# Two P V products of one head group joined into one block on TensorE, and two tile moves exchanged between ScalarE and VectorE

## The reference

```python
q = _layer_norm(query, ln1_g, ln1_b)
qh = (q @ wq + bq); kh = (context @ wk + bk); vh = (context @ wv + bv)
scores = jnp.einsum('bqhd,bkhd->bhqk', qh, kh) * scale
scores = jnp.where(allowed, scores, NEG_INF)        # causal
probs = jax.nn.softmax(scores, axis=-1)
o = jnp.einsum('bhqk,bkhd->bqhd', probs, vh)
x = query + o @ wo + bo
ff = jax.nn.gelu(_layer_norm(x) @ w1 + b1, approximate=False) @ w2 + b2
return x + ff
```

## Time and profile before

| what | value |
|---|---|
| median of 3 runs | 2777.89 us (2776.44 to 2778.57) |
| the profiled execution's own time | 2778.07 us |
| its span | 2776.2 us |
| PE, PEld (its weight loads), DVE, ACT, POOL busy | 98%, 90%, 74%, 60%, 32% |
| granted clock of PE over the span | 0.995 of full speed |

### The profile page before, as it was taken

The page is one execution under the profiler, slowest core; times in us unless marked ns, Lnnn a source line. Parts: engine busy times, 40 slices in busy tenths (PEclk is TensorE's granted clock), DMA queues, the critical chain, the costliest instruction groups (busy, mean ns, idle before and its releaser), DMA issues.

```text
span 2776.2 us, 67352 instructions
## 1 busy us (share of the span) xinstructions
PE 2730.1 (98%) x21928; PEld 2489.3 (90%) x21928; DVE 2041.0 (74%) x5205; ACT 1654.4 (60%) x4017; POOL 893.4 (32%) x842
## 2 busy tenths in 40 slices
PE   7999999999999999999979999999998999999999
PEld 6888888888888888888869999999998999999999
DVE  6777777777777777777698787787788566566556
ACT  5766667666676666766665656656556445444444
POOL 6657566575765656656510000000000000000000
PEclk9999999999999999999999999999999999999999
DMA  5233333333333323333243533534435433343342
GB/s 186 104 126 132 118 118 118 129 131 111 121 117 129 133 106 125 121 130 124 100 163 130 196 146 148 196 135 160 191 126 197 160 145 141 129 166 136 122 157 99
DMA packets 153084, 383.58 MB, mean 138 GB/s; under 512 B 13440, under 2 KB 17536, under 8 KB 144768
## 3 DMA queue, kind: packets, MB, share of 16 engines
q1 hardware_dynamic: 152960, 382.28, 37.1%
HBM read 172.51 MB, written 109.05 MB: 101 GB/s over the span
## 4 chain that ended last, share of the span: by engine, by line
PE 94%; DVE 2%; issue 2%; POOL 1%; ACT 1%; DMA 0%; SPq 0%; DVEq 0%; POOLq 0%; ACTq 0%
PE bank_d L495 19%; PE bank_t L525 11%; PE bank_s L1299 7%; PE bank_d L490 7%; PE bank_s L1300 6%; PE bank_s L1301 6%; PE bank_s L510 6%; PE bank_v L548 5%; PE bank_d L1299 5%; PE bank_d L1301 5%; PE bank_d L1300 5%; PE bank_v L1299 2%; PE bank_v L1300 2%; PE bank_v L1301 2%; PE bank_t L1299 1%
## 5 line engine op out<-in xcount | busy, mean ns | idle before, releaser
L862 ACT ACTIVATE sm<-sm,mins 128x128 f32<-128x128 f32 (+3 forms) x1024 | 572.0, 559 | 439.2 <-DVE mins L670 434.6
L989 POOL TENSOR_SCALAR sm<-sm,recips 128x128 f32<-128x128 f32 (+3 forms) x512 | 549.8, 1084 | 235.9 <-DVE recips L682 234.1
L670 DVE CUSTOM_DVE_ANT_0 sm<-bank_s,mask 128x128 f32<-128x128 f32 (+3 forms) x1024 | 474.3, 484 | 66.8 <-PE bank_s L510 64.0
L615 DVE COPY pT<-bank_t 128x384 f32<-128x384 f32 (+1 forms) x544 | 306.8, 564 | 210.6 <-PE bank_t L525 208.5
L1299 PE MATMUL bank_s<-w_hi,a_hi 128*128 128x256 f32 x1536 | 435.6, 284 | 2.1 <-DVE a_lo L1425 2.1
L1300 PE MATMUL bank_s<-w_lo,a_hi 128*128 128x256 f32 x1536 | 435.0, 283 | 0.0
L1301 PE MATMUL bank_s<-w_hi,a_lo 128*128 128x256 f32 x1536 | 434.9, 283 | 0.0
L525 PE MATMUL bank_t<-ident,sm 128*128 128x128 f32 x2560 | 412.8, 275 | 10.5 <-POOL sm L989 3.4
L525 PEld LDWEIGHTS bank_t<-ident,sm 128*128 128x128 f32 x2560 | 306.6, 140 | 92.3 <-issue 32.7
L1299 PE MATMUL bank_d<-b_hi,w_hi 128*128 128x256 f32 x1280 | 369.8, 289 | 14.0 <-ACT g L1726 7.7
L1301 PE MATMUL bank_d<-b_hi,w_lo 128*128 128x256 f32 x1280 | 364.3, 285 | 0.0
(11 more groups left out here) (161 smaller groups left out, 6550.2 us busy)
## 6 DMA issues: line engine op xcount, KB each, us to landing
stack<-st_hi SPq DMA_DIRECT2D x256, 256.0 KB, 2.4
stack<-st_lo SPq DMA_DIRECT2D x128, 256.0 KB, 2.4
xr<-x_scratch SPq DMA_DIRECT2D x64, 512.0 KB, 4.2
b_scratch<-b_hi SPq DMA_DIRECT2D x16, 1792.0 KB, 9.1
b_scratch<-b_lo SPq DMA_DIRECT2D x16, 1792.0 KB, 12.8
b_hi<-b_scratch SPq DMA_DIRECT2D x16, 1792.0 KB, 7.3
b_lo<-b_scratch SPq DMA_DIRECT2D x16, 1792.0 KB, 11.2
xt<-in_x SPq DMA_DIRECT2D x64, 256.0 KB, 2.7
```

The source lines that it names most:

```text
L615: copy(out, src).then_inc(moved[n % 2], 1)
L670: op = V.tensor_tensor_reduce(sm[:, n % SLOTS_S, off:off + w], bank_s[n % BANKS_S][:, off:off + w], mask[:, 512 - w:512], 1.0, 0.0, ALU.ad ...
L862: op = A.activation(row, row, ACT.Exp, bias=mins[:, g % 2, c:c + 1], scale=-1.0, accum_out=sums[:, g % 2, c:c + 1])
L989: op = G_.tensor_scalar(out=row, in0=row, scalar1=recips[:, g % 2, c:c + 1], scalar2=None, op0=ALU.mult)
```

## The change

P V of the second group leaves its two places. Both pairs are now done one after the other in step 3 of the third group (n = 27), after K3 and ahead of the transposes of tile 24. Steps 21 and 29 have no P V any more. The last tile of that group, tile 11 (n = 23, 512 columns), is moved in step 27 by DVE and no more by ACT; its tile 3 (n = 15, 384 columns) is moved in step 19 by ACT and no more by DVE. All other groups stay as they are.

```diff
-ACT_MOVES = [(5, 9, 11), (5, 9, 11), (3, 5, 7, 9, 11), (5, 9, 11)]
+ACT_MOVES = [(5, 9, 11), (3, 5, 9), (3, 5, 7, 9, 11), (5, 9, 11)]
...
-    R_AT, PV1_AT, PV0_AT, O_PROD_AT, O_HIGH_AT, O_HIGH_LATE = 4, 5, 9, 6, 7, 11
+    R_AT, PV1_AT, PV0_AT, PV_AT, O_PROD_AT, O_HIGH_AT, O_HIGH_LATE = 4, 5, 9, 3, 6, 7, 11
...
-                    if k == PV1_AT and not (it.first and g == 0):
+
+                    if k == PV_AT and g == 2:
+                        pv(it, g - 1, 0)
                         pv(it, g - 1, 1)
-                    if k == PV0_AT and not it.tail:
+                    if k == PV1_AT and g != 2 and not (it.first and g == 0):
+                        pv(it, g - 1, 1)
+                    if k == PV0_AT and g != 1 and not it.tail:
                         pv(it, g, 0)
                     if n >= LAG and not it.tail or n < LAG and not it.first:
                         p_transpose(it, n - LAG)
```

## The result

The changed kernel takes 2785.85 us (median of 8 runs, 2785.22 to 2790.05), the kernel before, run beside it, 2777.0 (8 runs, 2774.25 to 2778.57). The ratio is 1.0038, with a 95% interval of 1.003 to 1.0047: slower, by 8.9 us in the medians, where 9.4 had been forecast. The profiled executions lie 10.0 apart (2788.08 and 2778.07, spans 2786.2 and 2776.2).

A forecast was written before the change was run, and what follows sets the result against it. PE sets the pace (86.26 of 86.35 us a batch busy). 8.1 for batches 1 to 14, 1.5 for batch 0 and -0.2 for batch 15 give 9.4 on 2778.07, about 2787.3 us, 0.34% slower; range 2774.5 to 2792.

The forecast's parts named there:

- PE's own work: P V of both pairs: one joined block costs 2.445 us in place of 2.73, so PE alone gains 0.285 a batch.
- The moves exchanged at no cost: Steps 19 and 27: ACT's extra move (about 0.5) and DVE's (0.69) both fall into idle time and add nothing.
- Tile 24 late: Behind the joined block in step 27: the transposes of tile 24 come at 427.165 in place of 425.70.
- DVE's queue: From step 28: everything behind tile 24's move shifts by 1.465; the moves from tile 26 to tile 32's mask are 1.08 late.
- ACT's exponential of tile 32: It waits for DVE's mask of tile 32 and starts at 437.34 in place of 436.70, 0.64 late.
- DVE's `x_low` of X2: It waits for ACT's `x_high` of X2, so what follows it in DVE's queue is 0.64 late.
- the moves of tile 30 and 34: DVE's move of tile 30 and mask of tile 34, each 0.64 late, hold PE's transposes of tile 32 and scores of step 36.
- 0.58 a batch: Scores of step 36 start 0.52 to 0.64 later, taken as 0.58; over batches 1 to 14 it makes 8.1.
- Batch 0: 1.5 forecast: POOL's scalings hold PE in group 1, so emptying step 21 frees nothing: 0.58 + 0.93 = 1.5 lost.
- Batch 15: -0.2 forecast: No X blocks or statistics there, so at most 0.28 is gained, partly lost in PE's waits in its last group: -0.2.
- waits of 0.6 in L525 and 0.2 in L510: New PE waits for DVE in steps 35 and 36, on the move of `pT` and the mask, some 14 of each.
- The rival of the kept gain: The joined block's gain stays and DVE and ACT catch up unseen: -3.5 in all, 2774.4 us, chance 0.18.

The follow-up runs named there:

- join_stats3: The changed kernel with the next batch's fourth layer-norm statistics (about 1.15 us of DVE) in step 27 in place of step 28: 2773.43 us, 0.9987 of the kernel before.
- join_stats3_split: The changed kernel with the fourth statistics in step 27 and tile 24's transposes between P V of pair 0 and pair 1: 2776.63 us, 1.0006 of the kernel before.
- moves_only: The kernel before with only the two exchanged tile moves of the changed kernel, P V in its old places: 2774.8 us, 0.9996 of the kernel before.
- join_act26: The changed kernel with tile 26 of the third group moved by ACT in step 30 in place of DVE: 2782.68 us, 1.002 of the kernel before.
- stats3_only: The kernel before with only the fourth statistics in step 27 in place of step 28: 2776.03 us, 0.9999 of the kernel before.
- join_oldmoves: The changed kernel with the moves of tiles 3 and 11 given back to their former engines: 2789.24 us, 1.0042 of the kernel before.
- join_stats3_b0: The changed kernel with the fourth statistics in step 27 and batch 0's P V of pair 0 back in step 21: 2773.11 us, 0.9987 of the kernel before.

## Why the prediction was right, point by point

- **PE's own work: right.** Joined block 2.30, edges 0.33 and 0.30, step 21 shorter by 0.95. The mean period of join_stats3 over batches 1 to 14, where nothing stalls, is 86.07 against 86.37: the gain of 0.28 to 0.30 a batch is real, and join_stats3_split, which has the two switches back, loses it again.
- **The moves exchanged at no cost: right** for the time (moves_only).
- **Tile 24 late, DVE's queue, ACT's exponential of tile 32, DVE's `x_low` of X2, the moves of tile 30 and 34: right in each link.** 3.11 of idle time were expected as "nearly 3". The steps of the chain stand in the trace in the order and with the distances that were summed. Counted from the last product of step 21, the mask of tile 32 is 1.11 late (summed: 1.08), the exponential of tile 32 0.67, `x_low` of X2 and the move of tile 30 0.66 (0.64 each), the scores of tile 36 0.60 (0.58). Taking work off that chain (1.15 in join_stats3, 0.46 in join_act26) takes the loss away wholly and in part, though tile 24 is transposed as late as in the changed kernel. A rival in which PE would suffer from tile 24's lateness directly is excluded by this.
- **0.58 a batch: right in this place, short in the sum.** In batch 4 it is 0.60, and from the scores of step 21 to those of step 36 it is 0.61 in the mean of batches 1 to 14, 8.5 in all. The whole loss of these batches is 9.33 (from the joined block of batch 1, 166.59, to that of batch 15, 1385.10, against 154.78 to 1363.96 for P V in step 21 before), where 8.1 was forecast. Of the rest, 0.3 comes between step 36 and the end of the batch, 0.02 a batch; the kernels with the stall have it, join_stats3 doesn't, and what makes it is open. The other 0.5 lies in steps 0 to 2 and can't be told from scatter. There, PE's scores in step 2 wait up to 0.2 for DVE's mask, in different batches of each trace. From the list of waits, first the changed kernel and then the kernel before:

```profile
PEld bank_s L510 <- DVE mins L674: 0.4, 2, 0.2
```

```profile
PEld bank_s L510 <- DVE mins L670: 0.4, 2, 0.2
```

  These are batches 9 and 12 of the changed kernel, 2 and 14 of the kernel before. From the first scores of a batch to those of step 3, the 14 batches take 85.6 in all before and 86.1 in the changed kernel, but also 85.5 in moves_only and 86.2 in stats3_only, which lose nothing.
- **A reading of the kernel before was too smooth.** The periods of its batches 1 to 14 lie between 86.31 and 86.55, not within 0.1 of each other, and its weight loads do wait for DVE in the two places just shown. The sum by one batch held all the same, as batch 4 (86.33) has none of these waits.
- **Batch 0: 1.5 forecast, 1.4 measured.** From its first P V to the block of batch 1 it is 116.74 (49.85 to 166.59), before 104.50 to P V in step 21 and 10.81 from there to where the block would start. POOL's scaling held PE as said: PE's waits for it took over the place of the product that had left: from the scores of step 21 to those of step 22 it is 0.38 shorter, from there to those of step 27 0.33 longer.
- **Batch 15: -0.2 forecast, -0.27 measured** (34.18 from the block to the last P V of the stage, against 34.45).
- **Together:** 1.43 + 9.33 - 0.27 = 10.5 by the trace, against 9.4, of which an earlier start of this execution (49.85 against 50.28) takes 0.4, so that the two profiled executions differ by 10.0. The term that was too small is that of batches 1 to 14, by 1.2: 0.4 in the stall itself, 0.3 behind step 36, 0.5 in waits that scatter anyway.
- **Wrong in its shape:** I expected waits of 0.6 in L525 and 0.2 in L510, and none for X0. The trace shows 0.36, no wait in L510, and 0.2 at X0. The starts of the instructions tell more. The transposes of tile 32 come 0.84 after the scores of tile 35, in the kernel before 0.32 (to 440.40):

```profile
440.08 0.48 PE L510 MATMUL bank_s<-stack 128*128 128x512 f32 x1
```

  They are 0.52 late, of which the profile calls 0.36 idle, since it gives those scores a length of 0.48 though the next instruction can follow after 0.32. The scores of tile 36 come 0.38 after the transposes, before 0.24: they are 0.14 later still, right behind the mask of tile 34 (its end 443.91, their start 443.97), so that the second wait is there and only isn't listed. X0's wait costs nothing beyond: what follows is set by DVE. This is why PE counts as busy 86.56 of 87.01 while 0.60 are lost.
- **The rival of the kept gain** was the right forecast for another kernel: with the statistics moved, its 2774.4 is what join_stats3 gives within 1.

## What to carry to other kernels

Moving a long piece of the leading engine's work doesn't change its sum, but it makes a hole in the followers' input in one place and takes their catch-up time away in another. Follow the first instruction behind the hole through each in-order queue to the next point at which the leader needs something, subtract only the idle time that lies on that way, and compare with the slack there: here 1.74 of slack shifted, 0.6 came back as a loss, with no engine over 75% but the leader. If the hole can't be avoided, fill it: work in the follower's queue whose result is needed only later (here 1.15 of statistics) put into the hole turned +0.38% into -0.13%.

## What the runs showed of the hardware that was not expected

**A fall of the clock for a few microseconds in batch 0.** In the trace of join_stats3 the projections of step 24 of batch 0 start 0.43 apart in place of 0.23. Busy time by stretch for it, columns as in the earlier trace rows, with the granted clock of TensorE after that of POOL:

```profile
68.00:70.00 2.00, 0.85 (x6) 0.48 (x5) 1.80 (x8) 1.49 (x5) 2.00 (x3) 1.00 0.01 4
70.00:72.00 2.00, 1.67 (x10) 1.36 (x10) 1.46 (x8) 0.71 (x2) 2.00 (x2) 0.84 0.00 0
72.00:74.00 2.00, 2.00 (x8) 1.61 (x7) 1.73 (x8) 1.64 (x5) 1.98 (x3) 0.50 0.04 8
74.00:76.00 2.00, 2.00 (x12) 1.62 (x11) 0.16 (x1) 1.24 (x5) 2.00 (x2) 0.81 0.00 0
```

The changed kernel, the same stretch:

```profile
68.00:70.00 2.00, 1.16 (x7) 0.59 (x5) 1.80 (x6) 1.61 (x4) 2.00 (x2) 1.00 0.07 26
72.00:74.00 2.00, 2.00 (x14) 1.70 (x14) 2.00 (x10) 1.33 (x3) 2.00 (x2) 1.00 0.03 8
```

Behind the stretch in which PE waits for POOL, the clock stands at the lower of its two levels (0.50 of full speed, 1.2 GHz) for some 3 us, and step 24 takes about 1.4 longer. Of the ten traces, join_stats3, join_oldmoves and moves_only have it, the others with the same waits don't: what decides between them the traces don't show. The changed kernel has more of such waiting for POOL in batch 0 than the kernel before (4.1 against 3.4 by the list of waits), which may add such a fall to more of its runs; this was not measured.

**The start varies, and the faster first products make it longer.** The first P V of batch 0 comes at 46.4 to 46.9 in the traces of join_act26, join_stats3_split and join_stats3_b0, and at 49.5 to 50.3 in the seven others. The traces show where this arises. Rows of POOL, DVE and PE in the kernel before, one of the seven:

```profile
23.69 2.67 POOL L962 CAST cT_hi<-c_raw 128x512 fp32r<-128x512 f32 x1
23.39 2.50 DVE L722 TENSOR_TENSOR wv_lo<-sm,wv_hi 128x2048 fp32r<-128x2048 f32 x1
27.75 0.50 PE L495 MATMUL bank_d<-cT_hi,wk_hi 128*128 128x512 f32 x1 [3.00 <-POOL cT_lo L964]
```

Rows of POOL and DVE in join_act26, one of the three:

```profile
23.38 0.61 POOL L966 CAST cT_hi<-c_raw 128x512 fp32r<-128x512 f32 x1
25.27 2.28 DVE L726 TENSOR_TENSOR wv_lo<-sm,wv_hi 128x2048 fp32r<-128x2048 f32 x1
```

In the seven, PE's first projections start 0.23 apart. DVE so comes to its 128x2048 subtraction some 2 us earlier than in the three, at the time at which POOL casts the last part of the context: that cast takes 2.67 in all seven, and 0.61 in all three, where DVE's instruction comes behind it. PE then waits 3.0 for POOL, and behind this wait the granted clock is 0.50 (29 to 31 in the kernel before), so that the eight products of L443 take 4.60 (28.68 to 33.28) in place of 3.04 (26.30 to 29.34 in join_act26). In the three, the first projections start 0.43 apart until about 23, PE has no such wait, and no fall of the clock follows. (The profile gives a granted clock of 1.00 there from the first product on, though 0.43 apart is what products of this form show at 0.50 in step 24 above.) That the cast is slow because DVE works beside it fits all ten traces and was not tried by itself. What decides whether the first products go 0.23 or 0.43 apart the traces don't show.

The runs of the kernel before lie in two clusters, about 2774.3 and 2777.7, at the same distance. That these are the two starts is argued, not shown; it is why differences of 1 or 2 us are read here from distances inside a trace.
